# Attention and mixture-of-experts layer, head stage: the remainder's tile transposed by a DMA instead of TensorE, and the router one step later

## The chip, the cores and the metric

The kernel runs on the 8 cores of one Trainium2 chip. Every core runs the same program on its own sequence of 2048 tokens; nothing passes between the cores. The metric is the device time in microseconds of the slowest core, as a median over runs. The times that the profile shows for instructions are those of one profiled execution, of its slowest core (core 0).

## The reference, cut to what matters

x has shape (8, 2048, 1024). It is normalised, and an attention block and a mixture of 8 experts are both applied to the result and added to x:

```python
xn = _layernorm(x, axis=-1)
x = x + _L0_attn_ref(xn, ...) + _L0_ffn_ref(xn, Wr, We)

# attention (linear: softmax over the tokens of k, silu of q)
qkv = einsum('bnh,oh->bno', xn, w_qkv) + b_qkv
...
# experts: the router's logits decide which two experts a token goes to
logits = einsum('btd,ed->bte', xn, Wr)
top_vals, top_idx = top_k(logits, 2)
w = softmax(top_vals)
...
out = einsum('btk,btkd->btd', w, gathered)
```

The router's logits decide by comparison, so the kernel computes them more exactly than the rest: xn is split into a bf16 part xhi and a bf16 remainder lo, and Wr likewise.

## The kernel before, in words

The program is written as five lists of steps, one for each engine: TensorE (PE), VectorE (DV), ScalarE (AC), GpSimd (GP, "POOL" in the profile) and SyncE (SP, which only issues DMAs). Each list is played in order; a step can be preceded by waits for counters (class Lane, lines 43 to 119). The order in which build_nc appends steps is therefore the order on each engine, and a DMA that has to wait holds up what stands behind it in its engine's list.

The head (lines 517 to 559) works through 16 tiles of 128 tokens in a loop over s from 0 to 19. For a tile t:

- load_x (line 351, by SP) loads 128 rows of x, 512 KB in fp32, into one of four buffers xf. The load of tile t+4 is issued as soon as tile t has been normalised.
- h_stats (455): two bn_stats and a bn_aggr on VectorE. h_root (463): the square root on ScalarE. h_norm (468): two small VectorE steps, then ScalarE's normalisation of the tile (line 474, two buffers xnf), which also waits until the remainder of tile t-2 has been subtracted.
- h_hi (480): VectorE casts xnf to xhi (bf16, four buffers); POOL subtracts, lo = xnf - xhi (line 483, two buffers lo), and waits with trl(t-2) for the reader of the buffer's earlier contents; SP stores xhi to xn_d in HBM (line 485), from where the experts fetch it later.
- h_trans (488): eight TensorE transposes of 128x128 into one PSUM bank, then one VectorE copy of the bank to SBUF. It is called for xhi of tile s into xnT (line 547) and for lo of tile s-1 into xloT (line 556).
- h_v (495): eight matmuls for one half of the value projection of a tile (half 0 one step behind, half 1 four steps behind), each needing the copy into xnT (evh); ScalarE copies the result out (h_vout).
- h_router (506), two steps behind: eight matmuls with xnT and eight with xloT, small ones of 16 and 8 columns, into bank 7. The second eight wait for evl, the copy into xloT.

On TensorE a step of the loop is: h_v(s-1, 0), h_v(s-4, 1), eight transposes of xhi(s), eight of lo(s-1), h_router(s-2). On VectorE: cast to xhi(s), statistics of tile s+2, the two small steps for tile s+1, the copy into xnT, the copy into xloT. On SP: store of xhi(s), load of x tile s+5.

head_loads (400) starts the loads of the later weights from POOL's queue, with a cast from fp32: wk after tile 6, wq after tile 15, then two expert weights (lines 705 and 706). After the head come the k projection with softmax and the routing (k_proj, r_logits and following), the q projection and the attention output, the experts (m_step) and the output projection. r_logits (572) needs the last router result, and r_spread (661) writes over the head's buffers in stage, so it waits for all their readers.

The two calls that stand one behind the other at the end of a step:

```python
if 1 <= s <= NT:
    trl[s - 1], evl[s - 1] = h_trans(s - 1, lo[(s - 1) % 2], 2, xloT[(s - 1) % 2],
                                     lo_tok[s - 1], rt.get(s - 3))
if 2 <= s < NT + 2:
    h_router(s - 2)
```

Of the kernel before, what the change touches and what calls it, by code (L numbers as in the profile page):

```python
# [11 lines left out]
ALU = mybir.AluOpType  # L12
# [3 lines left out]
D = 1024  # L16
HC = 8
NT = 16
NB = 4
E = 8  # L20
# [101 lines left out]
def build_nc():  # L122
# [29 lines left out]
    with contextlib.ExitStack() as ctx:  # L152
        def sb(n, s, d):
            return ctx.enter_context(nc.sbuf_tensor(n, s, d))

        def counter(n):
            return Count(ctx.enter_context(nc.semaphore(n)))
# [4 lines left out]
        stage = sb("stage", [128, NT * D], BF16)  # L162
# [11 lines left out]
        def cut(region, at, n, d=BF16):  # L174

            k = 2 if d == F32 else 1
            a = region[:, at // 2: at // 2 + n * k]
            return a.bitcast(d) if d != BF16 else a

        KB = 1024  # L180
# [1 line left out]
        xf = [cut(wlate, (16 + i * 4) * KB, D, F32) for i in range(4)]  # L182
        xhi = [cut(stage, i * 2 * KB, D) for i in range(4)]
        lo = [cut(stage, (8 + i * 2) * KB, D) for i in range(2)]
        xloT = [cut(stage, (12 + i * 2) * KB, D).rearrange("p (c k) -> p c k", c=HC)
                for i in range(2)]
        xnf = [cut(stage, (16 + i * 4) * KB, D, F32) for i in range(2)]
        wvf = [cut(wring[2 - h], 0, HC * 512, F32).rearrange("p (c o) -> p c o", c=HC)
               for h in range(2)]
# [4 lines left out]
                                                                 c=NJE)  # L194
# [25 lines left out]
        wr_hl = sb("wr_hl", [128, HC, 2 * E], BF16)  # L220
# [77 lines left out]
        with nc.psum_tensor("PS", [128, 4096], F32) as PS:  # L298
# [8 lines left out]
            SP = Lane(ctx.enter_context(nc.semaphore("s_sp")))  # L307

            def mm(out, l, r, start, stop, *toks, sig=False):
                return PE.run(lambda e: e.matmul(out, l, r, start=start, stop=stop),  # L310
                              *toks, sig=sig)

            def tr(out, in_, *toks, sig=False):
                return PE.run(lambda e: e.transpose(out, in_, ident[:]), *toks, sig=sig)  # L314
# [8 lines left out]
            def tcopy(lane, out, in_, *toks):  # L323
                if lane is AC:
                    return AC.run(lambda e: e.copy(out, in_), *toks)  # L325
                return lane.run(lambda e: e.tensor_copy(out, in_), *toks)  # L326
# [37 lines left out]
            tk = {}  # L364
# [19 lines left out]
            def wv_cast(lane, h, c):  # L384
                t_wv[h, c] = tcopy(lane, wv3[0][:, c, 512 * h:512 * (h + 1)], wvf[h][:, c, :],
                                   wv_in[h, c // 2])
# [56 lines left out]
            lo_tok = {}  # L443
            evh = {}
            evl = {}
            trl = {}
            trh = {}
            xd_tok = {}
            rt = {}
# [13 lines left out]
            def h_root(t):  # L463
                s = t % 2
                sq[t] = act(sd[:, s:s + 1], mv[:, s, 1:2], AF.Sqrt, ag[t], t_const,
                            bias=eps_sb[:, 0:1])
# [21 lines left out]
            def h_trans(t, src, b, dst, tok, after):  # L488
                for c in range(HC):
                    p = tr(bankh[b][:, 128 * c:128 * (c + 1)], src[:, 128 * c:128 * (c + 1)],  # L490
                           tok, btok[b], t_idn, sig=(c == HC - 1))
                btok[b] = tcopy(DV, dst, bankh[b].rearrange("p (c k) -> p c k", c=HC), p, after)
                return p, btok[b]

            def h_v(t, h):
                b = 3 + 2 * (t % 2) + h
                for c in range(HC):
                    p = mm(bank[b], xnT[:, c, 128 * t:128 * (t + 1)],
                           wv3[0][:, c, 512 * h:512 * (h + 1)], c == 0, c == HC - 1,
                           t_wv[h, c], evh[t], btok[b], sig=(c == HC - 1))  # L500
                return b, p
# [4 lines left out]
            def h_router(t):  # L506
                lgt = bank[7][:, 16 * t:16 * (t + 1)]
                for c in range(HC):
                    mm(lgt, xnT[:, c, 128 * t:128 * (t + 1)], wr_hl[:, c, :], c == 0, False,
                       t_wrlo)  # L510
                for c in range(HC):
                    rt[t] = mm(lgt[:, 0:E], xloT[t % 2][:, c, :], wr_hl[:, c, 0:E], False,
                               c == HC - 1, evl[t], sig=(c == HC - 1))


# [7 lines left out]
            for s in range(NT + 4):  # L523
                if s < NT:
                    h_hi(s)
                if s == 0:
                    wv_cast(DV, 0, 2)
                    h_stats(1)
                    h_root(1)
                    wv_cast(DV, 0, 4)  # L530
                    wv_cast(AC, 0, 5)
                    trh[0], evh[0] = h_trans(0, xhi[0], 0, xnT[:, :, 0:128], hi_tok[0], None)
                    wv_cast(DV, 0, 6)
                    wv_cast(AC, 0, 7)
                if s == 1:
                    t_wrlo, t_iof = head_small()
                if s in (2, 3):
                    for c in range(4 * s - 8, 4 * s - 4):
                        wv_cast(AC, 1, c)
                if s + 2 < NT:  # L540
                    h_stats(s + 2)
                if s + 1 < NT:
                    h_norm(s + 1)
                v0 = h_v(s - 1, 0) if 1 <= s <= NT else None
                v1 = h_v(s - 4, 1) if s >= 4 else None
                if 1 <= s < NT:
                    trh[s], evh[s] = h_trans(s, xhi[s % 4], s % 2,
                                             xnT[:, :, 128 * s:128 * (s + 1)], hi_tok[s], None)
                if v0:
                    h_vout(s - 1, 0, *v0)  # L550
                if s + 2 < NT:
                    h_root(s + 2)
                if v1:
                    h_vout(s - 4, 1, *v1)
                if 1 <= s <= NT:
                    trl[s - 1], evl[s - 1] = h_trans(s - 1, lo[(s - 1) % 2], 2, xloT[(s - 1) % 2],
                                                     lo_tok[s - 1], rt.get(s - 3))
                if 2 <= s < NT + 2:
                    h_router(s - 2)
            t_wk, t_wq, t_wg = late["wk"], late["wq"], late["wg"]  # L560
            t_small = late["small"]
            t_xnT = evh[NT - 1]
            t_head_pe = rt[NT - 1]
            t_head_lo = evl[NT - 1]


            route = []
# [93 lines left out]
            def r_spread(lo_i, hi_i):  # L661

                def f():
                    q = slice(lo_i, hi_i)
                    tt(DV, hot_r[:, q, :], wide(prow[:, q], 128), tall(i_row[:], hi_i - lo_i),
                       ALU.is_equal, tk["place"], t_iof, t_head_pe, t_head_lo, trl[NT - 1],
                       lo_tok[NT - 1], *[xd_tok[t] for t in range(NT - 4, NT)])
                    tk["hc"] = tt(DV, hot_c[:, q, :], wide(ecol[:, q], NJE),
                                  tall(i_col[:], hi_i - lo_i), ALU.is_equal)
                return f  # L670
# [569 lines left out]
```

How the kernel before makes its waits and increments, by code:

```python
    def play(self, eng, steps=None, vals=None):  # L100
        for make, c, v in (self.steps if steps is None else steps):
            if make is None:
                eng.wait_ge(c.sem, v)
            elif isinstance(make, tuple) and make[0] == "read":
                vals = [eng.value_load(make[1][0:1, k:k + 1]) for k in range(E)]
            elif isinstance(make, tuple):
                _, key, floor, body, skip = make
                with eng.If(vals[key] > floor):
                    self.play(eng, body, vals)
                if skip:
                    with eng.Else():
                        for d, base, k in skip:
                            if base > 0:
                                eng.wait_ge(d.sem, base)
                            eng.sem_inc(d.sem, k)
            elif c is None:
                make(eng)
            else:
                make(eng).then_inc(c.sem, v)
```

## Time and profile before

| | |
|---|---|
| median of 3 runs | 585.56 us (585.11 to 586.95) |
| the profiled execution | 586.61 us |
| its span, slowest core (core 0) | 584.9 us |
| spans of the eight cores | 568.9 to 584.9 us |
| TensorE busy | 480.0 us (82%) |
| VectorE busy | 293.1 us (50%) |
| ScalarE busy | 209.7 us (36%) |
| POOL busy | 164.8 us (28%) |
| moved by DMA | 96.49 MB, mean 165 GB/s |

The span is the time from the first to the last instruction of the slowest core; the execution's own time has 1.7 us around it. In the profile PE is TensorE, PEld its loading of weights, DVE VectorE, ACT ScalarE, POOL GpSimd; SPq is SyncE's issuing of DMAs. Most matmuls go through one helper line (L310), transposes through L314, and the VectorE and ScalarE steps through helper lines too, so that the tile names (output<-input) tell the groups apart: xnt is xnT; stage holds xhi, lo, xloT and xnf; wlate holds xf; wr is a ring of weight buffers. Queue q1 is SP's, q0 POOL's and q10 ScalarE's. An entry in square brackets behind a row of the timeline is the engine's idle time before it, and what ended it.

### The profile page before, as it was taken

The page shows a single profiled execution, that of the slowest core. Times are in us where ns is not written, and L with a number is a line of the kernel's source. Part 1 is how long each engine was busy: PE and PEld are TensorE (multiplying, and loading weights), DVE is VectorE, ACT ScalarE, POOL GpSimd, SP SyncE. Part 2 cuts the span into 40 slices and gives each one's busy share as a digit, 9 for nine tenths or more (in the row PEclk, how much of TensorE's full clock was granted, in tenths as well). Part 3 has the DMA queues.
Part 4 walks back from the last instruction along what each step waited for, and adds up shares of the span by engine and source line. Part 5 has one row for each costly group of instructions (what it writes and reads, how often), then busy time and mean ns, then how long its engine had stood idle before and what let it go on. Part 6 is the DMA issues. An engine that isn't in the chain of part 4 may idle for free.

```text
span 584.9 us, 9174 instructions; the slowest of 8 cores (568.9 to 584.9 us)
## 1 busy us (share of the span) xinstructions
PE 480.0 (82%) x3104; PEld 244.8 (42%) x3104; DVE 293.1 (50%) x634; ACT 209.7 (36%) x337; POOL 164.8 (28%) x154
## 2 busy tenths in 40 slices
PE   0379999987778879997974858999975999999994
PEld 0145555444334444543433324444432444544441
DVE  3677674167885540456654544312110434455665
ACT  2164443353335524554543533442421332300000
POOL 2244336000091010101013374575742343210000
PEclk9889999999889979999995888999986999999998
DMA  7778963999504989600007373799999885358884
GB/s 208 194 238 226 214 208 65 165 164 166 93 1 136 287 196 175 108 1 1 1 1 145 70 167 96 143 244 168 219 246 259 226 280 149 153 180 259 262 292 194
DMA packets 37685, 96.49 MB, mean 165 GB/s; under 512 B 4416, under 2 KB 4544, under 8 KB 37632
## 3 DMA queue, kind: packets, MB, share of 16 engines
q0 software_dynamic: 18544, 44.37, 39.3%
q1 hardware_dynamic: 15552, 40.92, 22.9%
q10 hardware_dynamic: 3536, 10.52, 5.0%
q8 instruction: 30, 0.49, 0.3%
q14 instruction: 23, 0.19, 0.1%
HBM read 87.74 MB, written 31.46 MB: 204 GB/s over the span
## 4 chain that ended last, share of the span: by engine, by line
PE 56%; DMA 13%; DVE 12%; issue 9%; ACT 6%; DVEq 1%; POOL 1%; ACTq 0%; SPq 0%; POOLq 0%; PEldq 0%
PE PS L310 51%; DMA vq<-xn_d,tabs 6%; PE PS L314 5%; DMA wlate<-x_tm 5%; DVE nm L735 3%; DMA wr<-wv_t 2%; ACT stage L318 2%; DVE bst L875 2%; ACT vq L318 1%; DVE stage L334 1%; ACT ek L325 1%; DVE nb L334 1%; DVE stage L329 1%; ACT stage L325 1%; DVE wlate L329 1%
## 5 line engine op out<-in xcount | busy, mean ns | idle before, releaser
L310 PE MATMUL PS<-wr,xnt 128*128 128x512 bf16 x512 | 119.0, 386 | 12.1 <-DVE xnt L326 9.6
L310 PE MATMUL PS<-xnt,wr 128*128 128x512 bf16 x512 | 122.2, 386 | 0.5 <-ACT vq L318 0.5
L310 PEld LDWEIGHTS PS<-wr,xnt 128*128 128x128 bf16 x512 | 49.4, 99 | 71.8 <-issue 17.2
L310 PEld LDWEIGHTS PS<-xnt,wr 128*128 128x128 bf16 x512 | 48.4, 99 | 51.2 <-issue 4.4
L310 PE MATMUL PS<-wlate,stage 128*128 128x512 bf16 x288 | 68.4, 393 | 0.0
L314 PE MATMUL PS<-ident_sb,vq 128*128 128x128 bf16 x448 | 40.4, 234 | 25.3 <-DMA vq<-xn_d,tabs 15.0
L333 DVE TENSOR_SCALAR vq<-PS,wslot_f 128x512 bf16<-128x512 f32 x28 | 21.0, 751 | 78.5 <-PE PS L310 69.3
L310 PE MATMUL PS<-wr,stage 128*128 128x512 bf16 x224 | 52.4, 388 | 0.6 <-ACT stage L325 0.6
L325 ACT COPY stage<-PS 128x1024 bf16<-128x1024 bf16 x40 | 40.2, 1006 | 28.3 <-PE PS L314 25.5
L329 POOL TENSOR_TENSOR stage<-stage 128x1024 bf16<-128x1024 f32 x16 | 34.0, 2127 | 54.4 <-DVE stage L326 41.6
L314 PEld LDWEIGHTS PS<-ident_sb,vq 128*128 128x128 bf16 x448 | 30.4, 104 | 43.1 <-issue 37.2
L940 POOL DMA_INDIRECT vq<-xn_d,tabs x40 | 40.3, 1008 | 12.2 <-issue 11.3
L965 POOL DMA_INDIRECT eo_d<-vq,dtab x26 | 27.9, 1073 | 55.5 <-ACT vq L318 31.2
L310 PEld LDWEIGHTS PS<-wlate,stage 128*128 128x128 bf16 x288 | 28.5, 102 | 32.6 <-issue 4.6
L320 ACT ACTIVATE ek<-PS,nb 128x512 bf16<-128x512 f32 x32 | 22.0, 687 | 50.6 <-DVE nb L334 26.0
L318 ACT ACTIVATE stage<-wlate,nmr,rs 128x1024 f32<-128x1024 f32 x16 | 19.8, 1240 | 41.0 <-DVE nmr L334 40.9
L329 POOL TENSOR_TENSOR rs<-sd,half_sb 128x1 f32<-128x1 f32 x16 | 9.0, 561 | 89.8 <-DVE sd L333 89.8
L338 DVE SCALAR_TENSOR_TENSOR xnt<-stage 128x512 bf16<-128x512 f32 x32 | 22.2, 693 | 22.2 <-ACT stage L318 19.0
L314 PE MATMUL PS<-ident_sb,stage 128*128 128x128 bf16 x256 | 18.5, 229 | 17.9 <-DVE stage L326 13.8
L735 DVE TENSOR_REDUCE nm<-PS 128x1 f32<-128x512 f32 x32 | 22.1, 689 | 21.4 <-PE PS L310 21.2
L310 PEld LDWEIGHTS PS<-wr,stage 128*128 128x128 bf16 x224 | 21.8, 100 | 25.2 <-issue 2.9
L318 ACT ACTIVATE vq<-PS,wslot_f 128x512 bf16<-128x512 f32 x20 | 13.8, 688 | 51.0 <-PE PS L310 51.0
(146 smaller groups left out, 607.3 us busy)
## 6 DMA issues: line engine op xcount, KB each, us to landing
wlate<-x_tm SPq DMA_DIRECT2D x20, 512.0 KB, 6.7
eo_d<-stage SPq DMA_DIRECT2D x4, 2048.0 KB, 17.3
vq<-eo_d SPq DMA_DIRECT2D x16, 512.0 KB, 5.5
xn_d<-stage SPq DMA_DIRECT2D x16, 256.0 KB, 7.3
wlate<-we POOLq DMA_DIRECT2D x2, 2048.0 KB
wr<-we POOLq DMA_DIRECT2D x2, 2048.0 KB, 21.1
wlate<-we POOLq DMA_DIRECT2D x8, 512.0 KB
wr<-x_tm SPq DMA_DIRECT2D x8, 512.0 KB
```

What stands on the lines that cost most here:

```text
L310: return PE.run(lambda e: e.matmul(out, l, r, start=start, stop=stop), *toks, sig=sig)
L314: return PE.run(lambda e: e.transpose(out, in_, ident[:]), *toks, sig=sig)
L318: return AC.run(lambda e: e.activation(out, in_, func, bias=bias, scale=scale), *toks)
L320: return AC.run(lambda e: e.activation(out, in_, func, bias=bias, scale=scale, accum_out=acc), *toks)
L325: return AC.run(lambda e: e.copy(out, in_), *toks)
L329: return lane.run(lambda e: e.tensor_tensor(out, a, b, op), *toks)
L333: return lane.run(lambda e: e.tensor_scalar(out, a, s1, None, op0=op0), *toks)
L334: return lane.run(lambda e: e.tensor_scalar(out, a, s1, s2, op0=op0, op1=op1), *toks)
L338: return lane.run(lambda e: e.scalar_tensor_tensor(out, a, s, b, op0=op0, op1=op1), *toks)
L735: a = DV.run(lambda e: e.tensor_reduce(nm[:, j:j + 1], bank[bk], AX.X, ALU.max, negate=True), p)
L940: GP.steps.append((lambda e: e.indirect_dma_start(out=out, out_offset=None, in_=xn_d, in_offset=bass.IndirectOffsetOnAxis(ap=tabs[:, col:c ...
L965: GP.steps.append((lambda e: e.indirect_dma_start(out=eo_d, out_offset=bass.IndirectOffsetOnAxis(ap=dtab[:, col:col + 1], axis=0), in_=src ...
```

## The change

The lo tile is no longer transposed by TensorE. Behind the other work of step s, SP issues a DMA that reads lo(s) in SBUF and writes it transposed into xloT in SBUF. Its completion is both trl (lo may be overwritten) and evl (xloT is ready). VectorE's copy from PSUM goes with the transposes. There are four buffers xloT instead of two, each with a counter of its own, and h_router runs three steps behind instead of two.

```diff
-        xloT = [cut(stage, (12 + i * 2) * KB, D).rearrange("p (c k) -> p c k", c=HC)
-                for i in range(2)]
+        xloT = [cut(stage, at * KB, D).rearrange("p (c k) -> p c k", c=HC) for at in (12, 14, 24, 26)]
...
+            c_lt = [counter(f"c_lt{i}") for i in range(4)]
+
+            def h_turn_lo(t):
+                SP.after(lo_tok[t], rt.get(t - 4))
+                SP.steps.append((lambda e: e.dma_start_transpose(xloT[t % 4], lo[t % 2]),
+                                 c_lt[t % 4], 16))
+                trl[t] = evl[t] = SP.add(c_lt[t % 4], 16)
...
-                    rt[t] = mm(lgt[:, 0:E], xloT[t % 2][:, c, :], wr_hl[:, c, 0:E], False,
+                    rt[t] = mm(lgt[:, 0:E], xloT[t % 4][:, c, :], wr_hl[:, c, 0:E], False,
                                c == HC - 1, evl[t], sig=(c == HC - 1))
...
-                if 1 <= s <= NT:
-                    trl[s - 1], evl[s - 1] = h_trans(s - 1, lo[(s - 1) % 2], 2, xloT[(s - 1) % 2],
-                                                     lo_tok[s - 1], rt.get(s - 3))
-                if 2 <= s < NT + 2:
-                    h_router(s - 2)
+                if s < NT:
+                    h_turn_lo(s)
+                if 3 <= s < NT + 3:
+                    h_router(s - 3)
...
-            t_head_lo = evl[NT - 1]
...
                     tt(DV, hot_r[:, q, :], wide(prow[:, q], 128), tall(i_row[:], hi_i - lo_i),
-                       ALU.is_equal, tk["place"], t_iof, t_head_pe, t_head_lo, trl[NT - 1],
+                       ALU.is_equal, tk["place"], t_iof, t_head_pe, *evl.values(),
                        lo_tok[NT - 1], *[xd_tok[t] for t in range(NT - 4, NT)])
```

## Rows read from the trace of the kernel before

**Rows 1.** The page: the granted clock in 40 slices of 14.6 us.

```profile
PEclk9889999999889979999995888999986999999998
```

**Rows 2.** Stretches of 5 us: engines busy, then clock, DMA share, GB/s.

```profile
40.00:45.00 5.00, 4.32 (x32) 2.46 (x33) 3.54 (x9) 2.70 (x4) 2.58 (x2) 1.00 0.41 51
...
60.00:65.00 5.00, 4.78 (x50) 2.82 (x48) 3.56 (x8) 2.26 (x5) 2.12 (x1) 1.00 1.01 181
```

**Rows 3.** Timeline of one step: start us, us, engine, line, operation.

```profile
61.14 3.61 PE L310 MATMUL PS<-wr,xnt 128*128 128x512 bf16 x16 [0.22 <-ACT sd L318]
...
62.29 2.12 POOL L329 TENSOR_TENSOR stage<-stage 128x1024 bf16<-128x1024 f32 x1 [2.99 <-DVE stage L326]
...
64.11 1.24 ACT L318 ACTIVATE stage<-wlate,nmr,rs 128x1024 f32<-128x1024 f32 x1 [2.74 <-DVE nmr L334]
...
64.59 1.06 PE L314 MATMUL PS<-ident_sb,stage 128*128 128x128 bf16 x16
...
65.31 0.69 DVE L326 COPY xnt<-PS 128x1024 bf16<-128x1024 bf16 x1 [1.34 <-PE PS L314]
...
66.26 3.61 PE L310 MATMUL PS<-wr,xnt 128*128 128x512 bf16 x16 [0.22 <-ACT sd L318]
...
66.72 0.68 DVE L326 CAST stage<-stage 128x1024 bf16<-128x1024 f32 x1
```

**Rows 4.** The chain of waits: the sixteen transposes of a step.

```profile
85.27 0.89 PE PS L314 x16
```

**Rows 5.** Timeline at the start of the steady part.

```profile
39.74 0.68 DVE L326 COPY xnt<-PS 128x1024 bf16<-128x1024 bf16 x1
...
40.68 1.67 PE L310 MATMUL PS<-wr,xnt 128*128 128x512 bf16 x7 [0.90 <-DVE xnt L326]
```

**Rows 6.** DMA queues from 45 to 82 us: packets, MB, share of 16 engines.

```profile
q1 hardware_dynamic: 2544, 6.93, 58.3%
q0 software_dynamic: 1040, 2.10, 38.7%
...
wr<-wk_t POOLq DMA_DIRECT2D x1, 2048.0 KB, 28.0
```

**Rows 7.** Landing of the x loads issued at 60.31 and at 65.42 us.

```profile
DMA to landing us min/median/max: 13.2/13.2/13.2
...
DMA to landing us min/median/max: 13.3/13.3/13.3
```

**Rows 8.** Timeline where VectorE waits for x.

```profile
73.55 0.69 DVE L457 BATCH_NORM_STATS2 bst<-wlate 128x6 f32<-128x512 f32 x1 [1.24 <-DMA wlate<-x_tm]
...
76.49 3.61 PE L310 MATMUL PS<-wr,xnt 128*128 128x512 bf16 x16 [0.22 <-DVE xnt L326]
...
78.83 0.70 DVE L457 BATCH_NORM_STATS2 bst<-wlate 128x6 f32<-128x512 f32 x1 [0.98 <-DMA wlate<-x_tm]
...
80.72 0.68 DVE L326 COPY xnt<-PS 128x1024 bf16<-128x1024 bf16 x1
...
81.66 2.53 PE L310 MATMUL PS<-wr,xnt 128*128 128x512 bf16 x11 [0.28 <-DVE xnt L326]
```

**Rows 9.** Timeline at the end of the head.

```profile
98.20 2.12 POOL L329 TENSOR_TENSOR stage<-stage 128x1024 bf16<-128x1024 f32 x1 [0.73 <-DVE stage L326]
...
102.12 3.61 PE L310 MATMUL PS<-wr,xnt 128*128 128x512 bf16 x16 [0.22 <-DVE xnt L326]
...
106.42 1.89 PE L310 MATMUL PS<-wr,xnt 128*128 128x512 bf16 x8
...
108.56 3.61 PE L310 MATMUL PS<-wr,xnt 128*128 128x512 bf16 x16
```

**Rows 10.** Landing of the stores to xn_d issued at 87.8 and at 98.1 us.

```profile
DMA to landing us min/median/max: 2.1/2.1/2.1
...
DMA to landing us min/median/max: 9.1/9.1/9.1
```

**Rows 11.** Timeline, SP's queue where the first new DMA would follow.

```profile
24.37 0.33 SPq L78 DMA_DIRECT2D wlate<-x_tm  x1
```

## The prediction

> **What bounds the kernel now.** The profiled execution took 586.61 us, 1.05 us over the median of 585.56; my sum is made against it and the 1.05 us comes off at the end. The page first: TensorE is the busiest engine, and from about 35 to 110 us, where most of the change lies, it runs at the full granted clock, the 2.4 GHz level [rows 1]. So I read the head alone. By stretches, TensorE is busy 4.32 to 4.78 of each 5 us there, and the DMA engines are busy 0.41 of the time from 40 to 45 us and full (1.01) from 60 to 65 [rows 2]; a store issued at 87.8 lands within 2.1 us, so by then they are free [rows 10].
>
> Next the timeline of one step, to see what the 0.2 us idle in it is [rows 3]. The sixteen value matmuls (h_v) start at 61.14 and again at 66.26: a step is 5.12 us. In order on TensorE come 3.61 us of matmuls, eight transposes of xhi, eight of lo (0.89 us for the sixteen by the chain of waits [rows 4], so 0.44 us for eight), the router, and then the next h_v, which waits for VectorE's copy of the xhi transposes into xnT. That copy starts at 65.31 and takes 0.69 us; the matmuls start 0.26 us after its end. At the start of the head the same wait is plain: the copy at 39.74 ends at 40.42, and after 0.90 us idle, put down to this copy, the matmuls start at 40.68, again 0.26 us later [rows 5]. So each step is a loop of 3.61 (h_v) + 0.44 (transposes of xhi) + 0.12 (to the copy) + 0.69 (copy) + 0.26 = 5.12 us. The lo transposes and the router only fill the time in which TensorE would wait for the copy.
>
> Then who feeds the loop. From 45 to 82 us the two queues take 58.3% and 38.7% of all DMA engine time, 97% together [rows 6]: x loads and xn_d stores on SP's queue, and wk on POOL's, 28.0 us to land. The x load issued at 60.31 needs 13.2 us, that issued at 65.42 13.3 us [rows 7]. VectorE waits for both, and its copy into xnT stands behind the statistics in its order: after statistics started late at 73.55 the h_v of that step is still on time, after those at 78.83 the copy comes at 80.72, and the next h_v starts at 81.66, 5.17 us after 76.49 instead of 5.12 [rows 8]. On this core, the slowest, the x loads have no slack left at 79 us.
>
> **The change part by part.** *Removed from TensorE*: eight transposes in each of 16 steps, 0.44 us each. In the 13 steps of the steady part they go at nothing: the copy into xnT covers them, and TensorE waits 0.44 us longer for it. After the last h_v of half 0 (step 16) no xhi transpose and no such wait follows: there the eight lo transposes stood on the path between the matmuls that end at 102.12 + 3.61 = 105.73 and those that start at 106.42 [rows 9], so -0.4 us, once.
>
> *Removed from VectorE*: 16 copies PSUM to xloT of 0.68 us. Each stood behind the copy into xnT, and what it holds up is the cast to xhi of the next tile (66.72), which has until the next xhi transposes, at 66.26 + 3.61 = 69.9: no gain. In the first steps the casts wait for ScalarE's normalisation instead: none either.
>
> *The router one step later*: the same instructions, in the same gap; t_head_pe comes from router(15), now in step 18, with the last h_v of half 1 still to follow, so nothing is added to the end by the order. Four xloT buffers instead of two allow it, and the later r_spread waits name work long finished.
>
> *Added on SP's queue*: one DMA of 256 KB per tile, read and written in SBUF, issued behind a wait for lo_tok and for the router four tiles back. SP issues it after load_x(s+5) of the same step: the subtraction on POOL, 62.29 plus 2.12, ends at 64.41, before the load's issue at 65.42 [rows 3, 7], so SP's next store and load are not held. An issue of a plain copy takes 0.33 us of SP [rows 11], which has room; bounds 0.3 to 5 us for this one, the step being the most it may take unseen.
>
> Its price on the DMA engines is what no row shows. Low end: at the price per byte of SP's queue (58.3% of 37 us for 6.93 MB, 3.11 us per MB), 0.262 MB take 0.82 us of all 16 engines. High end: if each piece of 128 columns of one row (256 bytes, 1024 pieces, 64 per engine) costs a packet (58.3% of 37 us times 16, over 2544 packets: 0.136 us), 8.7 us. I take 1.5 us: the nearest row is a copy of the same bytes on the same queue, and the smaller pieces should cost something. The load issued at 65.42 has the four transposing DMAs issued from about 45 to 61 us ahead of it in the queue or sharing its engines, and the engines had 3% to spare: 4 x 1.5 = +6.0 us at the place with no slack (+3.3 at the low end). TensorE can't win it back afterwards, as its loop has no slack. Before 45 us I count nothing: the loads waited for there were issued before the first of the new DMAs, and from 40 to 45 us there is room. From 82 to 95 us there is room too: nothing.
>
> The Trainium skill, page "Advanced Engine Details and Errata", section "X-Bar Transpose (TRN2)", says that such DMAs are as fast as regular ones, at 350 to 400 GB/s. By it one would take 0.66 to 0.75 us, an estimate, and the term would be +2.8 us instead of +6.0. No row here shows one.
>
> *New waits.* POOL's subtraction of tile t+2 now waits until the DMA has read lo of tile t. The DMA issued at 65.8 has until the subtraction two steps behind 62.29, at 72.5: 6.7 us. If it lands after 13.3 us, as the x loads do, that subtraction ends at 81.2 instead of 74.6; who waits for it is ScalarE's normalisation two tiles further on (64.11 plus three steps, 79.5), and its cast has some 2 us of room before TensorE's transposes [rows 3]. So it just fits: 0, bounds 0 and +3 (behind it on SP: the wait for lo_tok, then the next store and x load). The router has three steps, some 14.8 us from issue: also just enough. At the end lo(15) is ready at 98.20 + 2.12 = 100.3 [rows 9], while wq and two expert weights fill the engines; the store issued at 98.1 took 9.1 us, the one at 87.8 2.1 us [rows 10]. A half-1 h_v with a router behind it takes 108.56 - 106.42 = 2.14 us here [rows 9]. TensorE is through with v(12) at 102.12 + 3.61 = 105.73 and comes to router(15) two such pairs later, at 110.0. A landing at 100.5 + 9.1 = 109.6 is in time; after 13.3 us, as the x loads of the full stretch, it would be at 113.8 and cost 3.8 us: I take +0.5, bounds 0 and +3.8.
>
> Sum: -0.4 + 6.0 + 0 + 0.5 = +6.1 us; 592.7 for the profiled execution, 591.7 for the median. What follows the head moves along with it.
>
> **The rivals.** A (hidden, not slower): the engine time called full is partly waiting for HBM, and an SBUF to SBUF transfer slips into it; the x load lands as before. For it: only two x loads are late by 1.2 and 1.0 us, and before 45 and after 82 us there is room. Against it: 97%, and loads in one ring stand behind each other. Then only -0.4 to +1 us remain, about 585.8. It turns to a loss once the four DMAs together cost over 0.4 us at 78.8.
>
> B (faster): TensorE's own work in a step, 3.61 + 0.89 and a router of 2.14 - 1.80 = 0.34 us, is 4.84 of the 5.12 us, and the 0.22 us idle before h_v may be its own sequencing, not the copy. Then 0.44 us go in 13 steps and 0.4 at the end, -6.2 us: 579.4. Against it stands the equal 0.26 us behind the copy in a step where TensorE plainly waited [rows 5] and in the full ones, and the 5.17 us step, in which the copy alone was late.
>
> C (the transposing DMA is dear): at 8.7 us plus 16 packets of 0.136 for load and store, SP's queue takes 10.9 us per step and sets the pace. Sixteen of them from 24.7 us on, behind the load at 24.37 [rows 11], end at 199 us, against 110.0: about +89 us, 674. For it: the packet price and the row pieces. Against: it is the bound at its extreme. The Trainium skill, page "VectorE: DVE Perf Modes", section "The three transpose paths", gives 1309 ns for a 128x128 block by DMA against 390 on TensorE; eight such in a row would be 10.5 us, an estimate, and side with C. TensorE's row here is 0.055 us a transpose, so the page's figures are not prices per piece in a stream.
>
> **How the numbers follow.** A measurement of this kernel can tell 0.3%, some 1.8 us, from no change. Forecast: 0.67, with its own range from 588 (0.82 us a DMA, no wait at the end) to 612 (3 us each in the full stretch, +12; the two new waits at their ends, +7; a few more late loads). A 0.16, B 0.07, C 0.10. The 80% range is 587 to 612: it leaves out B, C and most of A's lower half. Faster 0.07, same 0.16, slower 0.77.
>
> **What would show it.** In the changed kernel: steady steps still 5.12 us long, with the idle time before h_v grown from 0.22 to about 0.65 us and put down to the copy into xnT; the total wait of VectorE's statistics for x well over 2.2 us, x landings of 15 us or more between 55 and 80; steps of 6 to 8 us there; the first k_proj some 6 us later, and all later stages moved by the same. Steps of 4.7 us would make B right; steps of 5.12 throughout A; steps of 10 us with SP's queue at the top C. If TensorE waits at the router for the DMA, the new waits were undervalued.

## The result and the profile after

The changed kernel takes 607.2 us (median of 4 runs, 605.06 to 607.93) where the kernel before takes 585.6: 1.036 times as long, 95% interval 1.032 to 1.040. The direction was forecast, and the time lies in the stated range (587 to 612), but the size was not forecast: +6.1 us were expected and +21.6 came. Some executions of any kernel here fall into a slower state; the ratios below leave them out, and only the profile of e4, with its times in the table, is of such an execution.

The difference is made before the k projection starts. Its first matmul starts at 110.7 us before (mean of the eight cores, 109.1 to 112.0) and at 131.5 after (126.2 to 134.6): 20.8 us later. The starts of h_v on TensorE split them, as means of the eight cores (on cores 2 and 4 the record of a first matmul can be missing, 0.2 us). h_v(1, 0) starts 0.3 us later than before. From there to h_v(4, 0), the start of the head, it takes 16.4 us instead of 14.5; from h_v(4, 0) to h_v(15, 0), the last of half 0, 61.4 instead of 56.3; and from h_v(15, 0) to the first k_proj 23.6 instead of 9.9. So 1.8 us are lost at the start, 5.0 in the stretch behind it and 13.7 at the end.

The page of the changed kernel (the slowest core is core 6 here): packets, SP's queue and POOL's, and the chain of waits by line.

```profile
DMA packets 54580, 100.67 MB, mean 166 GB/s; under 512 B 21312, under 2 KB 21440, under 8 KB 54528
...
q0 software_dynamic: 18544, 44.37, 37.6%
q1 hardware_dynamic: 32448, 45.12, 26.4%
...
PE PS L309 46%; DMA stage<-stage 7%; DMA vq<-xn_d,tabs 6%; PE PS L313 5%; ACT stage L317 2%; DVE nm L740 2%; DMA wlate<-x_tm 2%; DMA wr<-wv_t 2%; DVE bst L880 2%; ACT vq L317 1%; POOL stage L328 1%; DVE stage L333 1%; ACT ek L324 1%; DVE nb L333 1%; SPq L78 1%
```

A new entry stands second in the chain: the transposing DMA (stage<-stage), 7%. Packets under 512 B were 4416 before: 16896 more, 1056 for each of the 16 DMAs, 66 on each engine. SP's queue takes 26.4% of 605.3 us where it took 22.9% of 584.9: 25.9 us more, 1.6 us of all engines for one DMA. That is a difference of two totals; one DMA alone can be read in e7, and there it takes 1.36 us. The 1.5 us of the forecast was a good figure; what it stood for was not.

The steady step, on TensorE: two starts of h_v, with the idle time before them.

```profile
54.17 3.61 PE L309 MATMUL PS<-wr,xnt 128*128 128x512 bf16 x16 [0.67 <-DVE xnt L325]
...
59.29 3.61 PE L309 MATMUL PS<-wr,xnt 128*128 128x512 bf16 x16 [0.67 <-DVE xnt L325]
```

5.12 us, as in [rows 3], with the idle time grown from 0.22 to 0.67 us and put down to the copy into xnT: the eight transposes went at nothing.

The first loss comes at the start of the head, before POOL's queue has any weight load (core 6):

```profile
25.33 6.36 SPq L498 DMA_TRANSPOSE stage<-stage  x1
...
36.94 2.13 POOL L328 TENSOR_TENSOR stage<-stage 128x1024 bf16<-128x1024 f32 x1 [9.04 <-DMA stage<-stage]
37.54 2.08 DVE L325 CAST stage<-stage 128x1024 bf16<-128x1024 f32 x1 [0.90 <-ACT stage L317]
...
42.36 5.20 PE L309 MATMUL PS<-wr,xnt 128*128 128x512 bf16 x16 [1.60 <-DVE xnt L325]
```

The DMA of tile 0, issued at 25.33, lands after 11.5 us (9.8 to 12.1 us on the eight cores), and its issue alone keeps SP 6.36 us. POOL's subtraction of tile 2, which writes the same lo buffer, starts only then. The next cast on VectorE, beside it, takes 2.08 us instead of 0.68, and TensorE's step from 36.90 to 42.36 takes 5.46 us. On core 6 of the kernel before, the same step takes 3.68 us:

```profile
34.10 1.89 PE L310 MATMUL PS<-wr,xnt 128*128 128x512 bf16 x8 [0.23 <-DVE xnt L326]
...
37.78 3.61 PE L310 MATMUL PS<-wr,xnt 128*128 128x512 bf16 x16 [0.52 <-DVE xnt L326]
```

The full stretch, in order of time, where the second loss arises:

```profile
58.34 2.38 SPq L498 DMA_TRANSPOSE stage<-stage  x1
...
66.10 7.73 SPq L498 DMA_TRANSPOSE stage<-stage  x1
...
75.60 2.12 POOL L328 TENSOR_TENSOR stage<-stage 128x1024 bf16<-128x1024 f32 x1 [13.02 <-DMA stage<-stage]
75.60 0.34 PE L309 MATMUL PS<-wr_hl,stage 128*128 128x8 bf16 x8 [1.84 <-DMA stage<-stage]
75.85 5.30 PE L309 MATMUL PS<-wr,xnt 128*128 128x512 bf16 x16
77.82 1.24 ACT L317 ACTIVATE stage<-wlate,nmr,rs 128x1024 f32<-128x1024 f32 x1 [8.66 <-POOL stage L328]
...
79.30 2.63 DVE L325 CAST stage<-stage 128x1024 bf16<-128x1024 f32 x1 [4.92 <-ACT stage L317]
...
82.07 0.61 PE L313 MATMUL PS<-ident_sb,stage 128*128 128x128 bf16 x8 [0.92 <-DVE stage L325]
...
84.66 3.61 PE L309 MATMUL PS<-wr,xnt 128*128 128x512 bf16 x16 [1.60 <-DVE xnt L325]
```

The DMA issued at 58.34 lands after 17.1 us, at 75.5. Both its waiters start then: POOL's subtraction, which wants to write lo again, and TensorE's router. ScalarE's normalisation waits 8.66 us for POOL, VectorE's cast 4.92 us for ScalarE, TensorE for the cast. The DMA issued next, at 66.10, keeps SP 7.73 us in its issue. The sixteen matmuls at 75.85 take 5.30 us instead of 3.61. By stretches the granted clock is 0.66 from 76 to 81 us, a mean that lies between the two levels, after TensorE had stood idle for 1.84 us; from 70 to 76 us it is 1.00.

And the end of the head: the last issue, the last router, the first k_proj; under them SP's and POOL's queue from 108 to 131 us.

```profile
107.97 5.90 SPq L498 DMA_TRANSPOSE stage<-stage  x1
...
131.22 0.35 PE L309 MATMUL PS<-wr_hl,stage 128*128 128x8 bf16 x8 [11.91 <-DMA stage<-stage]
131.43 3.31 PE L309 MATMUL PS<-wr,xnt 128*128 128x512 bf16 x8
134.58 3.62 PE L309 MATMUL PS<-xnt,wr 128*128 128x512 bf16 x16
...
q0 software_dynamic: 1757, 3.37, 87.6%
q1 hardware_dynamic: 1684, 0.64, 22.6%
```

TensorE waits 11.91 us at router(15) for one DMA of 256 KB, which lands 23.1 us after its issue. Every core has this wait, 10.9 to 12.4 us. The queues tell why: in these 23 us SP's queue moved 0.64 MB in 1684 packets and POOL's 3.37 MB in 1757: nearly packet for packet. The DMA of tile 14, issued at 103.17, stood in front of it and landed at 116.9, after 13.7 us. After the wait h_v(15) of half 1 runs at a granted clock of 0.58 (131 to 135 us), again behind an idle stretch.

### The profile page after: what moved, and what is told of

Read it like the earlier page. It is cut to its first block, busy times and chain, and to the rows that moved or that the text cites. A ratio compares the mean times of both kernels' runs of the same rounds, so it can differ in the third digit from the quotient of the medians.

```text
span 605.3 us, 8983 instructions; the slowest of 8 cores (586.3 to 605.3 us)
## 1 busy us (share of the span) xinstructions
PE 475.1 (78%) x2992; PEld 237.4 (39%) x2992; DVE 288.4 (48%) x620; ACT 210.0 (35%) x337; POOL 164.8 (27%) x154
## 3 DMA queue, kind: packets, MB, share of 16 engines
q1 hardware_dynamic: 32448, 45.12, 26.4%
## 4 chain that ended last, share of the span: by engine, by line
PE 51%; DMA 17%; DVE 12%; issue 10%; ACT 6%; POOL 2%; DVEq 1%; SPq 1%; ACTq 0%; PEldq 0%; POOLq 0%
PE PS L309 46%; DMA stage<-stage 7%; DMA vq<-xn_d,tabs 6%; PE PS L313 5%; ACT stage L317 2%; DVE nm L740 2%; DMA wlate<-x_tm 2%; DMA wr<-wv_t 2%; DVE bst L880 2%; ACT vq L317 1%; POOL stage L328 1%; DVE stage L333 1%; ACT ek L324 1%; DVE nb L333 1%; SPq L78 1%
## 5 line engine op out<-in xcount | busy, mean ns | idle before, releaser
L309 PE MATMUL PS<-wr,xnt 128*128 128x512 bf16 x512 | 123.9, 397 | 20.4 <-DVE xnt L325 18.5
L309 PE MATMUL PS<-xnt,wr 128*128 128x512 bf16 x512 | 120.6, 382 | 0.5 <-ACT vq L317 0.5
L309 PE MATMUL PS<-wlate,stage 128*128 128x512 bf16 x304 | 71.1, 389 | 0.2 <-ACT stage L324 0.2
L332 DVE TENSOR_SCALAR vq<-PS,wslot_f 128x512 bf16<-128x512 f32 x30 | 22.5, 750 | 78.2 <-PE PS L309 67.0
L324 ACT COPY stage<-PS 128x1024 bf16<-128x1024 bf16 x40 | 40.2, 1006 | 21.1 <-PE PS L313 20.8
L337 DVE SCALAR_TENSOR_TENSOR xnt<-stage 128x512 bf16<-128x512 f32 x32 | 22.2, 694 | 21.5 <-ACT stage L317 18.4
L317 ACT ACTIVATE vq<-PS,nmr,rs 128x1024 bf16<-128x1024 f32 x16 | 19.3, 1204 | 33.4 <-DVE nmr L333 33.4
## 6 DMA issues: line engine op xcount, KB each, us to landing
wlate<-we POOLq DMA_DIRECT2D x8, 512.0 KB, 11.8
```

The source lines that it names most:

```text
L317: return AC.run(lambda e: e.activation(out, in_, func, bias=bias, scale=scale), *toks)
L332: return lane.run(lambda e: e.tensor_scalar(out, a, s1, None, op0=op0), *toks)
L337: return lane.run(lambda e: e.scalar_tensor_tensor(out, a, s, b, op0=op0, op1=op1), *toks)
```

## The experiments

Theory 1, from this profile: an engine takes a packet from each queue in turn, so that the 66 small packets of a transposing DMA each wait for a large one of a weight load. Theory 2, the forecast's own: the DMA engines' total work is what counts. Theory 3, for the full stretch: SP's place in order, the blocked issue (a queue that is full, by the guess), holds the x loads. The kernel before was measured anew beside each group of runs and took 588 to 590 us there, so only ratios are compared, and beside them the start of the first k_proj (mean of eight cores of the profiled execution), 110.7 us before and 131.5 after. The last three columns say how much longer than before (14.5, 56.3 and 9.9 us) the start of the head, the stretch behind it and the end take, by the same starts of h_v as above; a dash stands where the order on TensorE is another.

| run | ratio to before (95%) | first k_proj, us | start | stretch | end |
|---|---|---|---|---|---|
| the change | 1.036 (1.032 to 1.040) | 131.5 | +1.8 | +5.0 | +13.7 |
| e1 late wq and expert weights | 1.013 (1.007 to 1.019) | 119.4 | +2.2 | +5.8 | -0.1 |
| e2 router late alone | 1.001 (0.998 to 1.005) | 112.1 | +0.4 | 0.0 | +0.4 |
| e3 / e12 xhi transposes between the halves | 0.994 (0.990 to 0.997) / 0.996 (0.992 to 1.000) | 108.5 / 108.4 | - | - | - |
| e4 four lo buffers | 1.036 (1.030 to 1.042) | 129.8 | +0.8 | +5.0 | +12.4 |
| e5 transposing DMA beside | 1.019 (1.012 to 1.027) | 122.6 | +1.8 | +9.5 | 0.0 |
| e6 plain copy beside | 1.008 (1.004 to 1.012) | 117.6 | +2.0 | +4.3 | 0.0 |
| e7 wk late too | one run, 1.025 | 123.0 | +2.2 | 0.0 | +9.3 |
| e8 three repairs | 1.005 (1.001 to 1.009) | 112.8 | - | - | - |
| e9 e1 and e4 | 1.013 (1.008 to 1.018) | 117.8 | +0.2 | +6.3 | -0.1 |
| e10 e9, x from ScalarE | 1.042 (1.035 to 1.048) | 132.4 | -0.6 | +21.2 | -0.1 |
| e11 hybrid | 0.993 (0.991 to 0.996) | 106.9 | - | - | - |

The start column tells what the first loss is. With a DMA that reads lo from two buffers it is 1.8 to 2.2 us, whether the DMA transposes or copies (the change, e1, e5, e6, e7) and whether wk is loaded early or late. With four buffers it is -0.6 to 0.8 (e4, e9, e10), and without the DMA 0.4 (e2). So it goes with the wait for the lo buffer, and no weight load is needed for it.

### The wait at the last router

```diff
-                    late["wq"] = w_load(2, wq_t, stat[t], *[t_wv[0, c] for c in range(HC)])
...
+            late["wq"] = w_load(2, wq_t, stat[NT - 1], evl[NT - 1],
+                                *[t_wv[0, c] for c in range(HC)])
```

The added lines stand behind the head's loop; the gate weights and the first two expert weights follow wq in POOL's order.

> The changed kernel, but wq, the gate weights and the first two expert weights are loaded only after the last transposing DMA has landed. Theory 1 (packets take turns: the 66 small packets per engine of one transposing DMA each wait for a large packet of the weight load): DMAs 14 and 15 land in 3 to 5 us instead of 13.7 and 23.1, TensorE's 11.9 us wait at the last router goes, and the kernel gains 11 to 13 us, to about 595. Theory 2 (the DMA engines' total work is the limit, so that the weight loads only move): the wait at the router goes but an equal one comes up at wq or at the experts, and the time stays within 3 us of 607.

Measured: 1.013 instead of 1.036. The last issues on SP, POOL's wq load and TensorE's end of the head (core 0):

```profile
108.61 1.23 SPq L496 DMA_TRANSPOSE stage<-stage  x1
...
112.18 0.91 POOL L78 DMA_DIRECT2D wr<-wq_t  x1 [3.71 <-DMA stage<-stage]
...
118.86 0.34 PE L309 MATMUL PS<-wr_hl,stage 128*128 128x8 bf16 x8
119.06 1.89 PE L309 MATMUL PS<-wr,xnt 128*128 128x512 bf16 x8
120.79 3.62 PE L309 MATMUL PS<-xnt,wr 128*128 128x512 bf16 x16
```

DMAs 14 and 15 land after 3.0 us each, TensorE passes the last router without a wait, and the first k_proj comes 12.1 us earlier. The loads, moved behind, cost nothing: theory 2 falls for this place. The 23.1 us were the company of POOL's queue.

### The router's step alone

```diff
-                                                     lo_tok[s - 1], rt.get(s - 3))
-                if 2 <= s < NT + 2:
-                    h_router(s - 2)
+                                                     lo_tok[s - 1], rt.get(s - 5))
+                if 3 <= s < NT + 3:
+                    h_router(s - 3)
```

> The kernel before with the second part of the change alone: router three steps behind instead of two, four xloT buffers, transposes on TensorE as before. Both theories: no difference, 585.6 within 1 us. If it is slower by several us, part of the loss belongs to the order and not to the DMA.

1.001, interval 0.998 to 1.005: no difference shown. The loss belongs to the DMA. In the trace the end takes 0.4 us more, 10.3 us instead of 9.9: one router more stands behind the last half-0 h_v. In the changed kernel that is set off by the eight lo transposes that are gone from there (e1 takes 9.8 us).

### Four buffers for lo

```diff
+        lo = [cut(stage, (8 + i * 2) * KB, D) for i in range(2)] + [ek[:, 0:D], ek[:, D:2 * D]]
...
-                               hi_tok[t], trl.get(t - 2))
+                               hi_tok[t], trl.get(t - 4))
```

> The changed kernel with four lo buffers instead of two, so that POOL's subtraction waits for the DMA of four tiles back. If the loss of some 8 us between 60 and 90 us comes through that buffer (subtraction 13.0 us late, then ScalarE, VectorE, TensorE), at least 5 of it go and the time is 599 to 602; what is left is the router's own wait of 2 to 5 us. If it comes from late x loads, as predicted, or from SP's long issue, the time stays at 605 to 607. The wait at the last router stays about 12 us in both.

The ratio did not move (1.036), but the waits changed place. On core 0 POOL waits 3.9 us for the DMA in the head instead of 32.2, but VectorE's statistics wait for x (4.0 us there, 2.8 to 9.0 on the others) and TensorE for the transposed tile. SP is held in one issue for 7.70 us (up to 13.7 on the other cores), and the x load behind it goes out late. The expected 5 us did not come: with the buffer's wait gone, two others are due almost as late. Only the start of the head gains, about 1 us.

### No weight load beside the head

The edit of e1, and wk behind the last transposing DMA as well:

```diff
-                if t == 6:
-                    late["wk"] = w_load(1, wk_t, stat[t], *[t_wv[1, c] for c in range(HC)])
+            late["wk"] = w_load(1, wk_t, evl[NT - 1], *[t_wv[1, c] for c in range(HC)])
```

> The changed kernel with no weight load of POOL's queue beside the head at all: wk, wq and the expert weights follow the last transposing DMA. Theory 1: every transposing DMA from 45 us on lands in 3 to 6 us, the subtraction never waits 2 us, all steps take 5.12 us, and TensorE reaches the last router at 108 to 112 us without a wait. The k projection then waits some 20 us for wk, so the whole is slower than the changed kernel by 5 to 12 us. If steps are still lost between 60 and 90 us, SP's issue or the x loads themselves are the cause.

The transposing DMAs from 43 us on, SP's queue from 97 to 100 us, when one such DMA is alone on the engines, and TensorE with the copy's wait, then with wk's:

```profile
L494 SPq DMA_TRANSPOSE stage<-stage x13: 1231/1233/2910, 43.6 to 101.8; - x13
...
DMA to landing us min/median/max: 3.0/4.0/8.4
...
q1 hardware_dynamic: 1056, 0.26, 45.3%
...
63.20 3.61 PE L309 MATMUL PS<-wr,xnt 128*128 128x512 bf16 x16 [0.67 <-DVE xnt L325]
...
68.31 3.61 PE L309 MATMUL PS<-wr,xnt 128*128 128x512 bf16 x16 [0.67 <-DVE xnt L325]
...
123.09 5.30 PE L309 MATMUL PS<-xnt,wr 128*128 128x512 bf16 x16 [8.97 <-DMA wr<-wk_t]
```

All steps from 50 us on take 5.11 to 5.15 us on the six cores whose matmul records are complete, and the stretch takes 56.3 us, as before: the loss in the full stretch needs wk beside it. TensorE is through with the head at 114.1 on this core, 113.7 in the mean, still 3 us later than before, and 2.2 of these are lost at the start, where the DMA of tile 0 lands after 10.3 us on this core with SP's queue alone at work. Landings from 43 us on reach 8.4 us, over the expected 6, and POOL waits 8.8 us for them in all, without an effect on TensorE. The DMA alone takes 45.3% of 3 us, 1.36 us of all engines. The wait for wk was 9 us instead of 20, since wk lands sooner when it is alone, and the whole came out at 603.92 us beside 589.4, 1.025 in a single run, under the changed kernel's 1.036 instead of 5 to 12 us over it.

### Small packets against the same bytes

The kernel before, all its TensorE work kept, with a DMA of lo beside it whose result nobody reads; the second run has `dma_start` in its place.

```diff
+            def h_side(t):
+                SP.after(lo_tok[t], trd.get(t - 2))
+                SP.steps.append((lambda e: e.dma_start_transpose(
+                    side[t % 2].rearrange("p (c k) -> p c k", c=HC), lo[t % 2]), c_lt[t % 2], 16))
+                trd[t] = SP.add(c_lt[t % 2], 16)
...
-                               hi_tok[t], trl.get(t - 2))
+                               hi_tok[t], trl.get(t - 2), trd.get(t - 2))
```

> The kernel before, with everything on TensorE as it was, and beside it the 16 transposing DMAs of lo into two spare buffers that nobody reads; POOL's subtraction waits for them before it writes lo again. Theory 1 (the small packets take turns with wk's large ones, and the late landing holds lo): the stall between 60 and 90 us comes as in the changed kernel (the subtraction waits 10 to 14 us once, 5 to 9 us lost), and the 12 us at the last router do not: 1.0 to 1.6% slower than before. A rival, that the loss comes from the missing TensorE transposes or the new router order: no difference to before.

> The same with a plain copy of the same 256 KB in place of the transposing DMA: rows of 2 KB, so 8 packets per engine instead of 66. Theory 1: in the full stretch it lands in 8 to 14 us like its neighbours, the subtraction is held by 6 us at most, and the loss is 0 to 3 us. Theory 2 (bytes and engine time count, 0.8 us against 1.6 us a DMA): about half of the loss of the transposing one, 3 to 4 us, with x loads as late.

From 50 to 80 us, first the transposing DMA, then the plain copy: issue time in ns (min, median, max), POOL's wait, landing.

```profile
L501 SPq DMA_TRANSPOSE stage<-stage x3: 1901/8122/10032, 51.6 to 70.7; - x3
...
  POOL stage L329: 23.7, 3
...
DMA to landing us min/median/max: 12.5/15.1/23.6
```

```profile
L501 SPq DMA_DIRECT2D stage<-stage x5: 470/471/1348, 49.7 to 77.2; - x5
...
  POOL stage L329: 8.0, 2
...
DMA to landing us min/median/max: 3.2/10.8/15.6
```

The transposing one costs 1.9% (1.2 to 2.7) without any work on TensorE having changed, a little over what was expected, and its head ends 11.9 us late. The plain copy missed its expectation: with 144 packets, 9 per engine, it still costs 0.8%, and its head ends 6.9 us late. At the start of the head both lose the same, 1.8 and 2.0 us. In the stretch behind it the copy loses 4.3 us and the transposing DMA 9.5. So nearly half of that loss needs no small packets: any reader of lo behind the x loads in SP's queue that lands up to 16 us after its issue (10.8 in the middle) comes too late where lo has two buffers. The other half comes with the transposing form. Whether it comes by the small packets, by the engine time or by the long issues on SP (up to 10.0 us in this window against 1.3) these two runs do not separate.

At the end of the head the two runs are a clean pair: no core waits there, SP and POOL issue the same DMAs in the same order, and DMA 15 goes out 0.2 us behind the first expert weights in both. Its landing, first transposing, then copying (core 0):

```profile
stage<-stage SPq DMA_TRANSPOSE x1, 22.9
...
stage<-stage SPq DMA_DIRECT2D x1, 256.0 KB, 9.4
```

On the eight cores it is 21.1 to 23.8 us against 8.2 to 10.6, and for DMA 14 11.2 to 14.5 against 2.7 to 3.2. The same bytes beside the same load: the difference of 13 us is the transposing form. Its longer issue on SP, 3.8 to 5.9 us for DMA 15, is part of it; its engine time, 1.36 us alone (e7), is far too small for it, so theory 2 falls for this place once more. The copy's 9.4 us are the 9.1 us that the forecast had read from a store.

### Whose place in order it is

```diff
-                    x_tok[t + 4] = load_x(t + 4, xnf_tok[t])
+                    x_tok[t + 4] = AC.move(c_x[t % 4], xf[t % 4],
+                                           x_tm[128 * (t + 4):128 * (t + 5), :], xnf_tok[t])
```

on top of late wq and four lo buffers.

> The changed kernel with late wq and four lo buffers: the base for the next run. The wait at the last router is gone; in the full stretch SP is held in the issue of one transposing DMA for 8 to 14 us, x loads issued behind it come late, and VectorE's statistics wait 4 to 9 us. 1 to 2% slower than before.

> The same, with the x loads of tiles 4 to 15 issued by ScalarE right behind the normalisation that frees their buffer, so that they stand neither in SP's order nor in its ring behind the transposing DMAs. Theory 3 (what holds the head in the full stretch is SP's place in order: the issue blocks when the ring is full, and x waits behind it): the statistics wait under 2 us in all, and of 6 to 10 us lost between 50 and 90 us only TensorE's own wait for the late transposed tile stays (2 to 6 us). Theory 2 (the DMA engines' total work): the x loads come as late as before and the time stays within 2 us of the base run.

The base ran nearly as expected: 1.013, the longest issue 6.9 to 13.1 us in the cores (13.12 on core 5), statistics waiting 2.7 to 13.7 us. The DMA of that issue and, below it, the DMA issued at 64.09 in the run with x from ScalarE and that run's waits of TensorE (core 7):

```profile
L496 SPq DMA_TRANSPOSE stage<-ek x1: 13119/13119/13119, 57.5 to 57.5; - x1
...
DMA to landing us min/median/max: 25.2/25.2/25.2
```

```profile
L497 SPq DMA_TRANSPOSE stage<-stage x1: 16370/16370/16370, 64.1 to 64.1; - x1
...
DMA to landing us min/median/max: 22.9/22.9/22.9
...
PE PS L309 <- DMA stage<-stage: 13.7, 1, 13.7
PE PS L309 <- DMA stage<-ek: 8.1, 2, 4.4
```

The statistics wait 3.2 us at most now, nearly as theory 3 had it, and yet the kernel is 3% slower than its base: TensorE waits 11.7 to 22.2 us for transposed tiles where 2 to 6 were expected. A third queue has joined, and the two transposing DMAs issued at 44.1 and 48.9 land after 20.7 and 35.8 us; one issue on core 1 keeps SP 21.32 us. The same bytes in another queue, and other losers: theory 2, which has no place for that, falls here too, and SP's order was only one of the waits that a late transposing DMA can turn into.

### Without the copy's loop

```diff
-                v1 = h_v(s - 4, 1) if s >= 4 else None
                 if 1 <= s < NT:
                     trh[s], evh[s] = h_trans(s, xhi[s % 4], s % 2,
                                              xnT[:, :, 128 * s:128 * (s + 1)], hi_tok[s], None)
+                v1 = h_v(s - 4, 1) if s >= 4 else None
```

> The kernel before with the xhi transposes put between the two halves of h_v, so that VectorE's copy into xnT runs beside the second half. If the loop through the copy sets the step (5.12 us, as the prediction says), the step becomes TensorE's own work, 4.84 us, and 13 steps gain up to 3.5 us unless the x loads come too late in the full stretch: 582 to 585. If the 0.22 us before h_v were TensorE's own sequencing, the step stays 5.12 and the time 585.6.

The same starts of h_v on TensorE, in the halves now:

```profile
50.83 0.34 PE L310 MATMUL PS<-wr_hl,stage 128*128 128x8 bf16 x8
51.03 1.89 PE L310 MATMUL PS<-wr,xnt 128*128 128x512 bf16 x8
...
55.78 1.89 PE L310 MATMUL PS<-wr,xnt 128*128 128x512 bf16 x8
```

The step is 4.75 us, without idle time, and the ratio 0.994 (0.990 to 0.997). In the full stretch one or two steps on each core take 5.0 to 6.2 us, as the x loads come too late there for the faster pace (on core 0 VectorE waits 1.90 us for one at 75.19). That VectorE's copy set the step of 5.12 us is shown; TensorE's own work is 0.09 us less than the 4.84 us that I had added up.

> The changed kernel with the three repairs together: late wq, four lo buffers, xhi transposes between the halves of h_v. Where the DMA engines are free a step takes TensorE's own 4.3 to 4.4 us; in the full stretch x loads and the router still wait, 4 to 8 us. Sum against before: 13 steps by 0.75 us gained, 4 to 8 lost, so between 6 us faster and 1 us slower; against the reordered kernel alone no better.

With three repairs (e1, e4 and this order) the changed kernel comes to 1.005 of before, 2.6 us slower where -6 to +1 was expected: the repairs take most of the loss away and leave no gain. A single stall between 58 and 73 us remains, some 9 us of TensorE's wait for the transposed tile on each core; one issue on SP takes 13.6 us in it.

> Tiles 0 to 10 of lo on TensorE, tiles 11 to 15 by the transposing DMA, when wk has landed; wq late; xhi transposes between the halves of h_v. Theory 1: no DMA meets a weight load, nothing waits, the steps of the last five tiles take 4.3 us in place of 4.75, and the kernel is 1 to 3 us faster than the reordered kernel alone, 5 to 7 us faster than before.

> The reordered kernel once more, on the chip of the hybrid: 0.993 of the kernel before, as measured; a step takes 4.75 us.

The hybrid is e1 with this order and:

```diff
-                if s < NT:
+                if 1 <= s <= NT and s - 1 < 11:
+                    trl[s - 1], evl[s - 1] = h_trans(s - 1, lo[(s - 1) % 2], 2, xloT[(s - 1) % 4],
+                                                     lo_tok[s - 1], rt.get(s - 5))
+                if 11 <= s < NT:
                     h_turn_lo(s)
```

Two starts of h_v(., 0) where the DMA serves:

```profile
86.23 1.89 PE L309 MATMUL PS<-wr,xnt 128*128 128x512 bf16 x8
...
90.53 1.89 PE L309 MATMUL PS<-wr,xnt 128*128 128x512 bf16 x8
```

4.30 us instead of 4.75, and TensorE shows no wait between them. The hybrid is 0.993 of before (0.991 to 0.996), the reordered kernel on the same chip 0.996 (0.992 to 1.000); its first k_proj comes 1.4 us earlier. Both are faster than both kernels; the hybrid's lead of 0.3% over the reordered one is not shown, as the intervals overlap.

## Why the prediction was right in direction and wrong in size

- *TensorE's transposes and VectorE's copy at nothing*: right in the steady steps. The step stayed 5.12 us, the idle time went to 0.67 us, and e3 shows that the copy was what bound it.
- *The router's later step at nothing*: nearly right by itself. The ratio of e2 shows no difference, but its trace has 0.4 us more at the end, where the forecast had "nothing is added". The order's wait at the end did not show until the DMA was late.
- *The DMA's price*: 1.5 us of engine time taken, 1.6 measured by totals and 1.36 alone. Its issue was given 0.3 to 5 us of SP; it takes 1.22 us at least and up to 8.05 in the changed kernel (core 1), 21.32 in e10.
- *Before 45 us, nothing*: wrong by 1.8 us. The forecast looked only at the x loads there. What waited was the lo buffer: the DMA of tile 0 landed after 9.8 to 12.1 us behind the x loads of its own queue, and with four buffers 0.2 (e9) to 0.8 us (e4) of the loss are left.
- *The full stretch, +6.0*: 5.0 us came, close in size, but by another way, so the agreement is luck. I had x loads late by the engine time of four DMAs. From 30 us on, VectorE's statistics wait for x 1.4 us or less on every core of the changed kernel; what waited was POOL (13.0 us at once on core 6), for the lo buffer. That wait stood in the forecast with the right deadline, 6.7 us, and with a landing of 13.3 us taken from the x loads, which "just fits"; the landing was 17.1. Even a plain copy, landing after up to 15.6 us, did not fit (e6). The lateness that I charged to x would have come second (e4, e9).
- *The end, +0.5 (0 to +3.8)*: the step that failed. It sized the landing of DMA 15 by a store of the same bytes at the same time, 9.1 us, and by an x load, 13.3 us. A copy or store of 256 KB has 9 packets on each engine (144 in all); this DMA has 66, nearly the 64 that the forecast itself had counted as the high end of the price, and then left out of the wait. It landed after 23.1 us, and TensorE waited 10.9 to 12.4 us for it, 11.8 in the mean, three times the upper bound of the term. A plain copy in its place lands after 9.4 us (e6), and with POOL's queue silent the transposing DMA lands after 3.0 (e1).
- *The drain, -0.4*: right, and readable before the wait. From h_v(15, 0) to the next h_v it is 3.86 us on core 6 (110.22 to 114.08) where it was 4.30 before (102.12 to 106.42 on core 0 [rows 9]), but the later router puts 0.4 us back behind it.

The sum of what came before the first k_proj is 0.3 + 1.8 + 5.0 + 13.7 = 20.8 us. The range held 607.2 because its upper end had been made of dear DMAs in the full stretch (+12) and both new waits; the wait at the end alone went past its own bound by 8 us and took up the room that the other terms left. That is luck too.

Not in the forecast was the clock. On core 6 the matmuls behind the waits of 1.84 and 11.91 us run at a mean granted clock of 0.66 and 0.58; the sixteen at 75.85 take 1.7 us more, the eight at 131.43 take 3.31 us instead of 1.89. The last is 1.4 of the 13.7 us at the end.

That the Trainium skill ("Advanced Engine Details and Errata", section "X-Bar Transpose (TRN2)") puts these DMAs at the speed of regular ones fits only roughly: alone this one takes 1.36 us of engine time (e7), against 0.82 for a copy of the same bytes at the queue's price, and beside another queue it does not fit at all (22.9 us against 9.4, e5 and e6). The 10.5 us worked out from the Trainium skill, page "VectorE: DVE Perf Modes", section "The three transpose paths", are too many for one alone: it lands after 3.0 us. The Trainium skill, page "DMA: Bandwidth & Descriptors", section "Queues, rings and completion order", says that an engine goes round its queues packet by packet; the 1684 to 1757 packets of the last stretch agree in kind. The page's packet holds several descriptors, and no run here shows whether the profile counts the same thing.

What stays open: how much of the landing in the full stretch is turn-taking and how much the queue in front of it. While the DMA of 58.34 was under way (58.4 to 75.4 us) SP's queue moved 1752 packets and POOL's 1040, so even turns alone don't give its 17.1 us. What holds SP in an issue is not shown either: theory 3's full ring is only argued, and at 25.33 us it held for 6.36 us with SP's queue alone at work. Whether transposing from HBM or in larger pieces would help was not tried.

## What to carry to other kernels

Size a DMA by two numbers, its engine time alone and its landing beside the queues that will be busy then, and take the second from a DMA with as many packets, not with as many bytes: a landing is what waits are made of. Before moving work from a busy engine to a DMA, find what the engine would otherwise wait for (here a copy whose loop, not the transposes, set the step), count how long each buffer that the DMA reads may stay taken, from the first tile on, and keep such a DMA away from bulk loads. If a prefetch can start later at no cost, as wq could, let it.

## What the runs showed of the hardware

- A transposing DMA of 128x1024 bf16 from SBUF to SBUF is 1056 packets under 512 B; alone it takes 1.36 us of the 16 engines (e7), 1.22 us of SP at the least, and lands after 3.0 us. A plain copy of the same bytes is 144 packets (e6).
- Beside POOL's weight loads it landed after 17.1 and 23.1 us in the changed kernel, where a plain copy in the last place took 9.4 us (e6); with three busy queues it took up to 35.8 us (e10, core 7), and SP stood in a single issue for up to 21.32 us (e10, core 1).
- Behind the x loads of its own queue alone it landed after 9.8 to 12.1 us, and its issue kept SP 4.9 to 7.2 us.
- Two queues with work shared the engines by packets, 1684 to 1757, and not by bytes, 0.64 to 3.37 MB, in the last stretch of the changed kernel; in its full stretch the packets were 1752 to 1040.
